# Second attention of a four-layer kernel: the low parts of keys and queries of batches 2 to 7 subtracted by GpSimd instead of VectorE

## What is computed

```python
Q = query @ Wq_w.T + Wq_b
K = key @ Wk_w.T + Wk_b
V = value @ Wv_w.T + Wv_b
...
energy = jnp.einsum('bhqd,bhkd->bhqk', Qh, Kh) * scale
attn = jax.nn.softmax(energy, axis=1)        # over the 16 heads, not over the keys
out = jnp.einsum('bhqk,bhkd->bhqd', attn, Vh)
...
return out @ Wo_w.T + Wo_b
```

## Time and profile before

| | |
|---|---|
| median of three executions | 1953.98 us (1951.7 to 1955.2) |
| the profiled execution, its own time | 1958.57 us |
| its span in the profile | 1956.8 us |
| PE busy | 1601.6 us, 82% |
| DVE busy | 1103.2 us, 56% |
| ACT busy | 831.6 us, 42% |
| POOL busy | 296.5 us, 15% |
| chain that ended last | PE 55%, DVE 24%, ACT 7%, issue 6%, DMA 5% |

### The profile page before, as it was taken

How to read it: one execution, slowest core, us unless ns; L and a number is a source line. 1 busy time by engine, 2 the same in 40 slices (tenths; PEclk the granted TensorE clock), 3 DMA queues, 4 the chain that set the end, 5 groups by cost and what they waited for, 6 DMA issues and landing times.

```text
span 1956.8 us, 29283 instructions
## 1 busy us (share of the span) xinstructions
PE 1601.6 (82%) x10374; PEld 1213.9 (62%) x10375; DVE 1103.2 (56%) x2538; ACT 831.6 (42%) x1851; POOL 296.5 (15%) x361
## 2 busy tenths in 40 slices
PE   5899872993888773578878999999879873999997
PEld 3566662882555542455544778787645452999997
DVE  5666628314899997866644353535469966222221
ACT  3455530323776642255545522212379941222221
POOL 1101100531121100111100000000102202233332
PEclk7899985997899986789989999999989975999999
DMA  7355234226553511544415000000456625522221
GB/s 160 50 83 77 45 127 171 43 38 126 119 111 84 102 36 46 76 63 69 67 23 239 2 1 1 1 1 17 71 70 107 105 85 197 159 38 35 34 38 27
DMA packets 86462, 144.08 MB, mean 74 GB/s; under 512 B 14299, under 2 KB 69987, under 8 KB 83139
## 3 DMA queue, kind: packets, MB, share of 16 engines
q1 hardware_dynamic: 66562, 102.86, 22.5%
q0 software_dynamic: 19776, 39.60, 12.8%
HBM read 75.50 MB, written 27.66 MB: 53 GB/s over the span
## 4 chain that ended last, share of the span: by engine, by line
PE 55%; DVE 24%; ACT 7%; issue 6%; DMA 5%; SPq 1%; POOL 0%; POOLq 0%; DVEq 0%; ACTq 0%
PE ps L1373 12%; PE ps L1481 7%; PE ps L1492 7%; PE ps L1342 4%; DVE probs L2218 3%; DMA Qpack<-QP 3%; PE ps L875 2%; PE ps L1254 2%; ACT pT L1618 2%; PE ps L1018 2%; PE ps L965 2%; PE ps L1263 2%; DVE hpart L2199 2%; PE ps L904 2%; PE ps L956 2%
## 5 line engine op out<-in xcount | busy, mean ns | idle before, releaser
L347 POOL DMA_DIRECT2D Kpack<-KP x192 | 101.3, 536 | 969.8 <-PE ps L1373 384.3
L1613 ACT ACTIVATE pT<-ps 128x512 f32<-128x512 f32 x256 | 151.7, 606 | 192.1 <-PE ps L959 98.7
L956 PE MATMUL ps<-Qpack,Kpack 99*128 99x256 bf16 (+1 forms) x768 | 166.5, 283 | 27.4 <-ACT pT L1618 11.6
L1481 PEld LDWEIGHTS ps<-xgT,XNT 128*128 128x128 f32 x1248 | 146.5, 193 | 1.9
L1481 PE MATMUL ps<-xgT,XNT 128*128 128x128 f32 x1248 | 146.7, 276 | 0.0
L1492 PE MATMUL ps<-w,mid 128*128 x624 | 141.0, 379 | 0.0
L925 PE MATMUL ps<-Kpack,Qpack 97*128 97x256 bf16 x512 | 103.6, 289 | 39.8 <-DMA Qpack<-QP 10.9
L1887 ACT ACTIVATE mid<-ps 128x512 f32<-128x512 f32 x78 | 42.4, 595 | 201.8 <-PE ps L1481 196.6
L1618 ACT ACTIVATE pT<-ps,nmax 128x256 f32<-128x256 f32 x256 | 121.0, 551 | 14.5 <-DVE nmax L2131 14.4
L2119 DVE CUSTOM_DVE_ANT_0 Vb<-ps,mask_bf 128x256 bf16<-128x256 f32 x256 | 95.0, 419 | 52.4 <-PE ps L925 52.3
L1492 PEld LDWEIGHTS ps<-w,mid 128*128 128x128 f32 x624 | 115.6, 190 | 14.1
(11 more groups left out here) (312 smaller groups left out, 3302.0 us busy)
## 6 DMA issues: line engine op xcount, KB each, us to landing
Kpack<-KP POOLq DMA_DIRECT2D x192, 128.0 KB, 5.0
Qpack<-QP SPq DMA_DIRECT2D x192, 128.0 KB, 6.0
w<-in_w SPq DMA_DIRECT2D x16, 1024.0 KB, 6.0
ctxT<-in_ctxT SPq DMA_DIRECT2D x32, 256.0 KB, 7.4
h_rows<-in_h SPq DMA_DIRECT2D x16, 512.0 KB, 6.4
h<-h_rows SPq DMA_DIRECT2D x2, 4096.0 KB, 22.2
wd<-in_wd SPq DMA_DIRECT2D x4, 1536.0 KB, 14.4
xn_rows<-xn SPq DMA_DIRECT2D x16, 256.0 KB, 2.4
```

What stands on the lines that cost most here:

```text
L347: eng.dma_start(Kpack[j][DH * k:DH * (k + 1)].rearrange("d (e f) t -> d e (f t)", f=HALF), KP[par][:, part]).then_inc(done, 16)
L956: mm = pe.matmul(A[h % ring][:, t], Kpack[par][0:rows, h, t * P:(t + 1) * P], Qpack[par][0:rows, h], start=True, stop=L != 0)
L1481: mm = pe.matmul(bank[:, f % 4 * P:(f % 4 + 1) * P], w1_tile[k % 2][:, c, f * P:(f + 1) * P], xgT3[k % 2][:, c], start=c == 0, stop=c == K ...
L1613: act.activation(pT[h % 8][:], A[h % 2][:], ACT.Exp).then_inc(s["exp_done"], 1)
```

## The change

For batches 2 to 7 of the second attention the functions `low_k` and `low_q` of DVE return at once, and POOL does the two subtractions instead. The one for keys (`low_key`) stands in POOL's queue just ahead of that batch's key pack, before the wait for `sc1_ps`, and waits for `k_mid`; the one for queries (`low_query`) stands right behind the six DMA issues of the pack and waits for `q_mid`. Both raise the same semaphores as before. Batches 0 and 1, and the other three attentions, are as they were.

```diff
             def attention(n, L):
                 i = order["att", L]
 
+                def low_key(b):
+                    pool.wait_ge(s["k_mid"], 8 * i + b + 1)
+                    pool.tensor_tensor(KP[b % 2][:, 2], kr[:], KP[b % 2][:, 1], ALU.subtract).then_inc(s["k_split"], 1)
+
+                def low_query(b):
+                    pool.wait_ge(s["q_mid"], 8 * i + b + 1)
+                    pool.tensor_tensor(QP[b % 2][:, 2], qr[:], QP[b % 2][:, 1], ALU.subtract).then_inc(s["q_split"], 1)
+
                 def pack_batch(b):
                     j = b % pack_ring(L)
+                    if L == 1 and b >= 2:
+                        low_key(b)
                     pool.wait_ge(s["k_split"], 8 * i + b + 1)
                     if L == 1 and b >= 2:
                         pool.wait_ge(s["sc1_ps"], exped1(2 * (b - 2) + 1, HPH - 1))
                     elif L != 1 and b >= PACK_RING:
                         pool.wait_ge(s["st_ps"], 16 * (8 * s_order[L] + b - PACK_RING + 1))
                     pack_keys(pool, j, b % 2, pack_k[j])
+                    if L == 1 and b >= 2:
+                        low_query(b)
...
                 def low_k(b, par):
+                    if L == 1 and b >= 2:
+                        return
                     dve.wait_ge(s["k_mid"], 8 * i + b + 1)
...
                 def low_q(b, par):
+                    if L == 1 and b >= 2:
+                        return
                     dve.wait_ge(s["q_mid"], 8 * i + b + 1)
```

## The result

| | before | changed |
|---|---|---|
| median of the first nine executions of each | 1954.16 us (1951.7 to 1960.28) | 1965.1 us (1954.4 to 1970.18) |
| ratio, first set | | 1.004, 95% interval 1.0021 to 1.006 |
| the changed kernel a second time, ten executions | 1955.21 us, of 33 | 1962.57 us (1953.21 to 1969.06) |
| ratio, second set | | 1.0037, interval 1.002 to 1.0054 |
| profiled execution, span | 1956.8 us | 1964.1 us |

A forecast was written before the change was run, and what follows sets the result against it. DVE was taken to bound the second attention: 4.8 us lost for keys plus 5.05 for queries, less 6.6 saved and 0.3 idle, gave 2.9 us on 1953.98, hence 1956.9 us, range 1948.0 to 1963.0.

The forecast's parts named there:

- The bound: Second attention: DVE, busy 19.66 of 20 us, sets the time until PE's slack of about 28.8 us is used up.
- The saving: Twelve subtractions leave DVE at 0.60 us each; one ahead of a 0.96 us wait saves nothing, leaving 6.6 us.
- The mechanism: A DVE instruction with two SBUF inputs and a POOL one do not run side by side; whoever comes second stands still.
- The size: Whole kernel: 2.9 us slower, 1956.9 us, with a range of 1948.0 to 1963.0 us.
- Keys: Key low parts on POOL, batches 2 to 7: DVE loses three times 0.8, twice 1.05 and once 0.3, 4.8 us.
- Queries: Query low parts on POOL behind the DMA issues: DVE loses five times 0.95 and once 0.3 us, 5.05 us.
- Idle time: DVE's 0.3 us of idle time behind unit 2 is filled by the loss at batch 2 and taken off.
- Rival A: No standing still, or hardly any: DVE and POOL share and DVE keeps the 6.6 us, 1947.4 us; chance 0.14.
- Rival B: POOL loses most races and gets in only at reciprocals and PSUM reads, half the hits vanish: about 1952 us; chance 0.11.
- Rival C: Batch 2's queries land late, PE's reader starts 4.9 us late and DVE stands 3.4 us: 1960.3 us; chance 0.20.
- Rival D: Mixed types make POOL's subtraction 2 us instead of 1.28, 8.4 us more: 1965 us; chance 0.05.
- sum of 8.8 us: High end: every one of the twelve subtractions costs DVE its whole 1.28 us, less the 6.6 us saved.

The follow-up runs named there:

- e1: Low parts of keys and queries of batches 2 to 7 left out altogether, on DVE and POOL, against the kernel before: 1947.94 us, ratio 0.9973.
- e7: Changed kernel plus a small POOL memset and semaphore wait between the DMA issues and the query subtraction: one execution, 1958.45 us against 1953.97 before.
- e5: Changed kernel with each of POOL's twelve subtractions replaced by a memset of an unused tile: ratio 0.9964 against the kernel before, stage 230.0 us.
- e4: Changed kernel with POOL's query subtraction moved ahead of the six DMA issues, behind the keys' one: ratio 1.0006 against the kernel before, stage 240.2 us.

## Why the prediction was right or wrong, point by point

**The bound.** Right. DVE sets the stage: with the twelve subtractions gone it is 7.2 us shorter and PE still waits for `m` (e1), and that wait is 28.9 us in the changed kernel, as in the earlier trace rows. At one place it did not hold, see the idle time below.

**The saving.** Right, 11 x 0.60 = 6.6 us. The subtraction ahead of the 0.96 us wait saves nothing: the wait is 1.56 us without it (e1, and the changed kernel). The 7.2 us of e1 hold 0.3 us of a wait that is gone, which the prediction took off on its own, and 0.3 us of small steps, which it had not.

**The mechanism.** Right, and it was the sign of the whole. The pair of small products in the earlier trace rows had shown it in another stage, and it came true for eleven of twelve. Of the earlier trace rows only a part bears on it: the DVE instruction at 1643.88 is a TENSOR_SCALAR with one tensor input, and the 1.25 us more of POOL's second product fit a wait until 1643.96, for the DVE product before that.

**The size.** Too small by nearly half. The forecast was 2.9 us; the stage lost 5.2 us and the kernel 7.2 to 7.8 us. On the median of the prediction the two ratios give 1961.2 and 1961.8 us, inside the range of 1948.0 to 1963.0; the median of the first nine executions, 1965.1, lies outside it. Term by term:

- Keys: 4.8 us forecast, 4.7 measured. The sum is luck: batches 3 and 6, given 1.05 us each, cost 0.74 and 0.84, and batch 7, given 0.3 us because of the reciprocal, cost 0.84.
- Queries: 5.05 us forecast, 6.6 measured. This is the mis-sized term. It took 0.95 us for a hit in the chain of dependent steps, 0.2 us less than a whole one, because the hand-over gap would be hidden; the hits cost 1.11 to 1.63 us. No gap was hidden, and DVE was held from the start of its own instruction on, up to 0.60 us ahead of POOL's record; e7 shows the cause. The 0.14 us of start-up did hold: 1.17 - 0.14 = 1.03 us, and the stalls are the lead plus 1.03. That batch 7 would be nearly free and batch 5 would not was the wrong way round.
- Idle time: the 0.3 us taken off are right, but a new wait of 0.95 us, in no term, came at 709.32 (DVE's timeline, changed kernel):

```profile
709.32 0.69 DVE L2200 TENSOR_TENSOR M<-S 128x1024 bf16<-128x1024 bf16 x1 [0.95 <-ACT S L1647]
```

DVE waits there for a copy of scores, hence for PE. PE was busy throughout 698 to 703 us at a granted clock of 0.50, its lower level; in the matching stretch of the kernel before, 690 to 695 us, the clock was 0.74. That the lower clock makes the wait is likely but not shown.

The sum is 4.7 + 6.6 - 6.6 - 0.3 + 0.95 = 5.35 us, less about 0.1 us of small steps: 5.2 us, as measured. About 1.6 us behind the stage, at a lower granted clock, was in no term. The kernel's loss is above the forecast for both reasons, and the rivals C and D, which held most of the chance on this side, had no part in it.

**Rival A**, no standing still: refuted for the subtractions. It is true for memsets (e5). **Rival B**, POOL loses most races: it lost seven in e4, but each time only until the end of one DVE instruction, and DVE's next one with two inputs paid 0.83 to 0.96 us. Losing spares DVE the cost only where a reciprocal comes next, as in batch 2 of e7. **Rival C**, the late query pack of batch 2: the pack was issued 4.35 us behind the first key DMA as worked out, but landed in 6.5 us at most, and nobody waited. The slower result has thus another cause than the rival on that side. **Rival D**: refuted, 1.17 us.

**The rule of the Trainium skill** (SBUF — State Buffer, "SBUF: two separate sides"): an exclusive lock for the whole instruction, against a DVE instruction with two SBUF inputs only where GpSimd's reads SBUF. The e5 run agrees, 230.0 us with memsets against 242.4 with subtractions. Whether the reading decides, as the rule has it, e5 can't tell from the kind of instruction. The prediction's sum of 8.8 us was not the rule to the letter, since the rule spares a DVE instruction with one SBUF input: it let the query part of batch 5 go free beside statistics. For the stage (5.2 us) it was further off than mine, for the kernel (7.2 to 7.8 us) nearer. A full 1.17 us for each of twelve would be 14.0 us; the stalls are 11.3 us. Two of them, 1.59 and 1.63 us, are longer than POOL's whole 1.17 us, which a lock held for the recorded length of the instruction doesn't give.

## What to carry to other kernels

Before elementwise work goes from a saturated DVE to GpSimd, look up what DVE will run at that moment: against an instruction that reads two SBUF tensors the move costs DVE about GpSimd's whole instruction, 0.7 to 1.6 us here against 0.60 us saved. Put it beside reciprocals, statistics or reads of PSUM, by a semaphore of DVE itself; eight of the twelve subtractions, placed like this, gained 0.3%. And don't let it stand right behind DMA issues of the same engine.

## What the runs showed of the hardware that I had not expected

A subtraction queued on POOL behind its own DMA issues held DVE up to 0.6 us before the record of the subtraction began: a DVE step of 0.42 us took 2.05 us beside 1.16 us of POOL. The issues alone don't do this (e5), nor does a subtraction that has to wait for a semaphore first (e7, longest query stall 0.99 us). With no issue ahead of it, POOL coming second stands until the DVE instruction under way has ended and then gets in before the next, even where DVE's instructions follow on each other without a gap (seven times in e4). Its record shows that wait as its own length, up to 3.11 us, and DVE's stalls are in DVE's recorded lengths too, not in its idle time.
